# First attention layer of a four-layer kernel: queries, keys and values in one product, a ring of three values, the norm chain two steps into a group

## The reference

```python
qkv = (xin @ Wqkv.T + qkv_bias).reshape(Bs, Lx, 3, H, D)     # H = 16 heads of D = 32
...
sm = jnp.exp(jnp.minimum(scale_mul_log, jnp.log(jnp.float32(100.0))))
qn = q / jnp.maximum(jnp.linalg.norm(q, axis=-1, keepdims=True), 1e-12) * sm
kn = k / jnp.maximum(jnp.linalg.norm(k, axis=-1, keepdims=True), 1e-12)
scores = jnp.einsum('bhqd,bhkd->bhqk', qn, kn) + attn_bias
p = jax.nn.softmax(scores, axis=-1)
o = jnp.einsum('bhqk,bhkd->bhqd', p, v)
...
x = x + attn(_ln(x) * (scale1 + 1.0) + shift1) * gamma1
```

## Time and profile before

| | us |
|---|---|
| median of 3 runs | 2710.25 (2709.88 to 2712.95) |
| profiled execution | 2711.11 |
| its span | 2709.3 |
| TensorE busy | 2364.4 (87%) |
| VectorE busy | 1540.6 (57%) |
| ScalarE busy | 1278.9 (47%) |
| GpSimd busy | 923.5 (34%) |

### The profile page before, as it was taken

One profiled execution on the slowest core, in us unless ns is written; L12 is line 12 of the kernel. 1 busy time (PEld: TensorE's weight loads), 2 busy tenths in 40 slices (PEclk: granted clock), 3 DMA queues, 4 the chain that ended last, 5 costly groups with the idle time before them and its releaser, 6 DMA issues. The chain is left out here.

```text
span 2709.3 us, 45585 instructions
## 1 busy us (share of the span) xinstructions
PE 2364.4 (87%) x15672; PEld 1931.5 (71%) x15672; DVE 1540.6 (57%) x4470; ACT 1278.9 (47%) x3188; POOL 923.5 (34%) x988
## 2 busy tenths in 40 slices
PE   7899999987699997788888788898899999996777
PEld 5787787876578885566666566777788888884565
DVE  5877777785634344656557366547543333334766
ACT  4677777776311112577677366656511111112443
POOL 0344443433767665123323023323111112112331
PEclk8799999999899998677877899999999999997998
DMA  6000000001100002000000100000100000001000
GB/s 258 1 2 6 5 5 6 5 10 45 65 16 32 31 0 73 36 32 1 1 1 2 43 1 1 1 1 1 48 24 24 24 24 23 0 0 51 8 24 32
DMA packets 17084, 65.26 MB, mean 24 GB/s; under 512 B 3292, under 2 KB 4060, under 8 KB 12276
## 3 DMA queue, kind: packets, MB, share of 16 engines
q1 hardware_dynamic: 16884, 62.70, 6.4%
HBM read 57.42 MB, written 5.28 MB: 23 GB/s over the span
## 5 line engine op out<-in xcount | busy, mean ns | idle before, releaser
L2004 POOL TENSOR_TENSOR l2m_hidl<-l2m_hid,l2m_hidh 128x512 fp32r<-128x512 f32 x64 | 100.9, 1577 | 445.6 <-DVE l2m_hidh L1974 445.6
L1869 ACT ACTIVATE l2m_gate<-l2m_psG 128x512 f32<-128x512 f32 x64 | 38.3, 598 | 437.0 <-PE l2m_psU L1800 436.2
L1150 ACT ACTIVATE l0a_prob<-l0a_prob,l0a_nmin 128x512 f32<-128x512 f32 x256 | 184.9, 722 | 58.7 <-DVE l0a_nmin L1431 58.3
L1969 DVE TENSOR_TENSOR l2m_hid<-l2m_gate,l2m_psU 128x512 f32<-128x512 f32 x64 | 44.0, 688 | 281.9 <-ACT l2m_gate L1869 281.9
L1626 POOL TENSOR_TENSOR l0a_prob<-l0a_prob,l0a_rinv 128x512 f32<-128x512 f32 x64 | 67.0, 1047 | 401.9 <-DVE l0a_rinv L1438 401.9
L1162 ACT ACTIVATE l0a_PT<-l0a_psT 128x512 f32<-128x512 f32 x256 | 152.8, 598 | 72.3 <-PE l0a_psT L982 61.7
L1431 DVE CUSTOM_DVE_ANT_0 l0a_prob<-l0a_psS,l0a_mask 128x512 f32<-128x512 f32 x256 | 175.2, 688 | 0.6 <-issue 0.6
L2024 POOL TENSOR_TENSOR res_X<-res_X,l0m_share 128x512 f32<-128x512 f32 x128 | 162.1, 1294 | 24.1 <-DVE l0m_share L1958 22.9
L835 PE MATMUL l0a_psA<-res_l0a_wh,res_hTh 128*128 128x128 f32 (+1 forms) x512 | 151.5, 296 | 19.0 <-ACT l0a_qT L1144 6.8
L1873 ACT ACTIVATE l0m_hid<-l0m_psG,l0m_b1c 128x512 f32<-128x512 f32 x64 | 43.9, 690 | 262.7 <-PE l0m_psG L1800 262.7
L982 PE MATMUL l0a_psT<-res_ident,l0a_prob 128*128 128x128 f32 x1024 | 160.5, 280 | 1.2 <-ACT l0a_PT L1162 0.8
(11 more groups left out here) (410 smaller groups left out, 7642.6 us busy)
## 6 DMA issues: line engine op xcount, KB each, us to landing
res_l2m_stage<-in_l2m_w SPq DMA_DIRECT2D x8, 1536.0 KB, 6.3
res_l0m_stage<-in_l0m_w SPq DMA_DIRECT2D x8, 1024.0 KB, 4.9
cond_w<-in_wmod SPq DMA_DIRECT2D x6, 1024.0 KB, 15.8
res_X<-in_x SPq DMA_DIRECT2D x4, 1024.0 KB, 12.0
l1a_wmod<-in_wmod SPq DMA_DIRECT2D x4, 1024.0 KB, 6.1
out<-res_X SPq DMA_DIRECT2D x16, 256.0 KB, 2.0
l_stage<-in_l_w SPq DMA_DIRECT2D x3, 1024.0 KB, 7.2
cond_stage<-in_l0a_w SPq DMA_DIRECT2D x3, 768.0 KB, 13.8
```

What stands on the lines that cost most here:

```text
L1150: act.activation(prob[:, n % NP, 0:w], src[:, 0:w], ACT.Exp, bias=nmin[:, n % NP:n % NP + 1], scale=-1.0, accum_out=ssum[:, n % NP:n % NP ...
L1969: v.tensor_tensor(hid[:, m, :], gate[:, m, :], psU[m][:], ALU.mult).then_inc(hid_done, 1)
L2004: pool.tensor_tensor(hidl[:, s % 2, m, :], hid[:, m, :], f32(hidh[:, s % 2, m, :]), ALU.subtract).then_inc(hl_done, 1)
```

## The change

Queries, keys and values of a tile become one product of 384 columns. It is cut into two jobs, the first two blocks of channels and the last two, so `proj` has eight halves a group, and both halves use one bank. ScalarE copies 256 columns to `raw` and 128 to `V`, tile by tile. `V` gets three slots, and a copy to a slot waits until the group that used it has been weighed. The tables are new: the halves stand at 7, 7, 8, 8, 11, 11, 16, 16 (group 2), 23, 24, 25, 25, 26, 27, 32, 32 (group 3), 39, 39, 40, 41, 42, 43, 48, 48 (next group 0) and 55, 55, 56, 57, 57, 58, 58, 59 (next group 1). `START` now makes all of groups 0 and 1. The norm chain's bias, squares and sums stand at steps 2, 3 and 4 of every group. The squares go to a tensor of their own place, which lies over `stack`, and wait for the transposes of keys that read it. `xn` holds one tile of rows, and the layer norm's tiles stand at 33, 36, 39 and 42. VectorE drains before each residual.

```diff
-    NORM0 = 7 if L is L0 else LAG + 1
-    NORM_T = (0, 1, 2, 3) if L is L1 else (0, 1, 3, 4)
+    NORM0 = 1 if L is L0 else LAG + 1
+    NORM_T = (0, 3, 6, 9) if L is L0 else (0, 1, 2, 3) if L is L1 else (0, 1, 3, 4)
...
-    VS = 2
+    VS = 3 if L is L0 else 2
...
-        XS = NT if is1 else 2
+        XS = 1 if is0 else NT if is1 else 2
...
+            sq = S.at("sq", [P, NT, QKW], F32, nc.sbuf_base - 4 * NT * SL * NSH * SW)[:]
...
-            sq = xn[:].rearrange("p r c -> p (r c)").rearrange("p (t w) -> p t w", w=QKW)
...
+        PROJ_AT = {2: (7, 7, 8, 8, 11, 11, 16, 16), 3: (23, 24, 25, 25, 26, 27, 32, 32),
...
+        def v_slot(b, hg):
+            return (b * NG + hg) % VS if is0 else hg % VS
...
+        def halved(job):
+            return job[0] == "out" or is0 and job[0] == "proj"
...
-                            sp.wait_ge(v_mm, 2 * NG * B)
...
-                def project(b, hg, t, ps):
-
+                def project(b, hg, x, ps):
+
+                    t, half = divmod(x, 2) if is0 else (x, 1)
...
-                        mm = product(ps, 0, 256, t, lambda w, k: w3(w, hg % NG * GW, 384, k)[:, 0:256])
+                        mm = product(ps, 0, 384, t, lambda w, k: w3(w, hg % NG * GW, 384, k),
+                                     range(2 * half, 2 * half + 2))
...
-                    mm.then_inc(proj_done, 1)
+                    if half:
+                        mm.then_inc(proj_done, 1)
...
-                        freed[i] = [(raw_done, NRAW * (g if is0 else bn) + (x + 1))]
-                    elif kind == "v":
-                        project_v(hg, x, psA[i])
-                        freed[i] = [(v_done, 2 * g + (x // 2 + 1))]
+                        freed[i] = [(v_done, NT * g + (x // 2 + 1)) if is0 else (raw_done, NRAW * bn + (x + 1))]
...
                         act.activation(raw[:, t, hg % 2, :], ps[:, 0:QKW], ACT.Copy).then_inc(raw_done, 1)
+                        if t == 0 and g >= VS:
+                            act.wait_ge(pv_done, U // NG * (g - VS + 1))
+                        act.activation(V[:, v_slot(b, hg), t, :], ps[:, QKW:QKV], ACT.Copy).then_inc(v_done, 1)
...
-                        v.wait_ge(v_mm, 2 * NG * b)
+                        v.wait_ge(proj_done, NT * NG * b)
...
+                    if not start:
+                        v.wait_ge(kT_mm, 4 * (b * NG + hg))
...
+                        v.drain()
                         v.tensor_tensor(xn[:, t % XS, :], ps[:], G[:], ALU.mult)
...
-                        p = s - (2 if hg == NG else 0)
-                        if p == 1:
+                        if s == 2:
                             qk_bias(b, hg)
-                        if p == 2:
-                            qk_squares(hg)
-                        if p == 3:
+                        if s == 3:
+                            qk_squares(b, hg)
+                        if s == 4:
                             qk_norms()
```

More of the change, by code:

```diff
@@ L597, in attention @@
         out_mm, out_done, g_in, xg_done = (S.sem(n) for n in ("out_mm", "out_done", "g_in", "xg_done"))
[L598 to L599 removed]
+        ck_mm, ckh_done, ckl_done, v_done = (S.sem(n) for n in ("ck_mm", "ckh_done", "ckl_done", "v_done"))
         chunks = split_chunks(WCOLS)
@@ L679, in jobs @@
             if hg < NG:
-                if is0 and n in PROJ_AT and (more or PROJ_AT[n][0] < NG):
-                    todo.append(("proj", *PROJ_AT[n]))
-                if is0 and n in V_AT and (more or V_AT[n][0] < NG):
-                    todo.append(("v", *V_AT[n]))
+                if is0:
+                    todo += [("proj", g, x) for g in PROJ_AT if more or g < NG
+                             for x, at in enumerate(PROJ_AT[g]) if at == n]
                 if not is0 and more and hg == NG - 1:
@@ L712, in jobs @@
             return todo
-        START = (([] if PRE else [("norm", 0, t) for t in range(NT)]) + [("proj", 0, t) for t in range(NT)]
+        START = (([] if PRE else [("norm", 0, t) for t in range(NT)])
+                 + [("proj", 0, x) for x in range(2 * NT if is0 else NT)]
                  + ([("ck", 0, 0)] if is1 else [])
-                 + ([("v", 0, t) for t in range(NT)] + [("proj", 1, t) for t in range(NT)] if is0 else
+                 + ([("proj", 1, x) for x in range(2 * NT)] if is0 else
                     [("kv", 0, 0), ("kv", 0, 1)] + ([("far", 0, 0)] if is1 else []))
@@ L720, in attention @@
             START += [("q", 0, j), ("k", 0, j)] if is0 else [("q", 0, j)]
+        def halved(job):
+            return job[0] == "out" or is0 and job[0] == "proj"
         def second(job):
-            return job[0] in ("v", "out") and job[2] % 2 == 1
+            return halved(job) and job[2] % 2 == 1
         def with_banks(todo, last=1, held=None):
@@ L735, in with_banks @@
                     last = 1 - (last if held is None else held)
-                    held = last if job[0] in ("v", "out") else held
+                    held = last if halved(job) else held
                 out.append((job, last))
@@ L829, in latent, with product @@
                     mm.then_inc(ck_mm, 1)
-                def product(ps, c0, n, t, cols):
-                    for k in range(NK):
+                def product(ps, c0, n, t, cols, ks=range(NK)):
+                    for k in ks:
                         for i, (l, r) in enumerate(passes(hTh, hTl, wh, wl)):
@@ L1001, in weigh @@
                             else:
-                                v, rows = V[:, hg % VS, qt if is1 else c, v0:v0 + HD], P
+                                v, rows = V[:, v_slot(b, u // NT), qt if is1 else c, v0:v0 + HD], P
                             mm = pe.matmul(psO[o][row:row + HD, qt * P:(qt + 1) * P],
@@ L1046, in norm_evacuate, with raw_copy @@
                     op.then_inc(hf_done, 1)
-                def raw_copy(b, hg, t, ps, start):
-                    g = b * NG + hg
+                def raw_copy(b, hg, x, ps, start):
+                    g, t = b * NG + hg, x // 2 if is0 else x
                     act.wait_ge(proj_done, (NT * g if is0 else NRAW * (b + (1 if hg == NG else 0))) + (t + 1))
@@ L1121, in run @@
                         act.activation(ckh[:], psA[i][:], ACT.Copy).then_inc(ckh_done, 1)
-                    elif kind == "proj":
+                    elif kind == "proj" and (second(job) or not is0):
                         raw_copy(b, hg, x, psA[i], start)
-                    elif kind == "v" and second(job):
-                        act.wait_ge(v_mm, 2 * g + (x // 2 + 1))
-                        act.activation(V[:, hg % VS, x - 1:x + 1, :],
-                                       psA[i][:, 0:2 * P].rearrange("p (t c) -> p t c", t=2),
-                                       ACT.Copy).then_inc(v_done, 1)
                     elif kind == "kv":
@@ L1291, in qk_bias, with qk_squares @@
                                     qb[:, None, w_hg * P:(w_hg + 1) * P].to_broadcast([P, NT, P]), ALU.add)
-                def qk_squares(hg):
+                def qk_squares(b, hg, start=False):
+                    if not start:
+                        v.wait_ge(kT_mm, 4 * (b * NG + hg))
                     v.drain()
```

16 lines of the change are left out of this document (4 added, 12 removed).

## The result

Measured: 2720.17 us (median of 5 runs, 2718.84 to 2722.35) against 2709.88 for the kernel before (5 runs). The ratio is 1.0041, with a 95% interval of 1.0028 to 1.0054: slower by 10 us, where 20 us less were forecast. The profiled execution took 2721.5 us, its span 2719.7, mean clock 0.913 (before 0.921). The attention layer runs from 42.0 to 683.2 us, 12 us more than before; the later layers gave about 2 back, which is within what repeated runs differ by: from the last score product of this attention to the end the profiles of this case took 2059.5 to 2068.3 us, with the same instructions.

The account below looks back on a forecast made before the run. TensorE was taken to bound the kernel, some 25 us a batch ahead of the next engine. 2 x -7.1 - 4.6 - 6.5 + 1 + 4 = -20.3 us, from 2711.1 to 2690.8; own range 2680 to 2702, range given 2673 to 2707.

Parts of the forecast that it names:

- TensorE's saving: Joined products: 384-column matmuls 0.174 us apart, a tile 2.09 us instead of 2.76, 43 us less over 64 tiles.
- rival C: Matmul spacing goes by columns, so the wide one costs what two narrow did, 0.230; products only change places: 2711; chance 0.03.
- Where the removed work lay: Groups of a middle batch: product time -4.7, +2.7, -5.2, -3.4 counted as -3.5, +2, -3.6, -2, together -7.1 us.
- the three signs of being wrong: Spacing 0.2 or more; batches 1 and 2 over 145 us; half clock in more than one stretch of a batch.
- Before the first batch: Start: wide matmuls on the slow clock delay VectorE's bias 2 us, partly offset by less TensorE work before transposes: +1 us.
- The small edits: Bias place, narrow value copies, bank, drains, value slot and weight transfer: together +4 us.
- the bias wait: VectorE at step 2 of a group waits for ScalarE's copy, 11 times: bounds 0 and 11 us, 1 us extra counted.
- the drain's 0.1 each: VectorE's drain ahead of each of the 16 residuals costs 0.1 us, 1.5 us in all.
- the bank's 0.5 a batch: Bank freed one copy later; jobs at steps 40, 42, 44 take the bank just filled: 0.5 us a batch, 1.5 in all.
- B: VectorE takes it all: bias waits add 11 us, group 2 stays at 42 us; together 22, so 2712; chance 0.12.
- A: TensorE stays the bound throughout and all 43 us come: about 2668; chance 0.08.
- D: Granted clock falls in eleven product-free heads of groups 0, 2 and 3, 3 us each, 33 in all: 2724; chance 0.07.

Follow-up runs that it names:

- the second run of the second set against the first: Kernel before with 384-column products at the old query and key places, later values unused: 2715.63 us; the same with spread norm and residual drains: 2716.07 us.
- the run with 2 of 12 matmuls: Changed kernel, each joined tile after those ahead of the first batch issuing only 2 of its 12 matmuls (results wrong, copies and waits kept): 2692.88 us.
- the fill: Changed kernel with each first-layer score product issued three times in steps without a job, to keep TensorE's clock up: 2716.24 us.
- the four-slot version: Changed kernel with four value slots, half products spread over more steps and the kernel before's narrow start, nothing left out: 2701.62 us.
- the run without the chain: Changed kernel without VectorE's squares, sums, roots and scaling of queries and keys after the first group, TensorE's instructions untouched: 2668.97 us.

## Why the prediction was wrong

**TensorE's saving: right.** Spacing 0.174, a tile 2.09. Columns alone (rival C) would have made the join worth nothing; it is worth 23.7 us in place. The group sums of product time (-4.7, +2.7, -5.2, -3.4) were right as well.

**Where the removed work lay: the step that failed.** It turned the work of a whole group of 16 steps into time with a discount: -3.5, +2, -3.6, -2 and so -7.1 a middle batch, and it had no term for the clock. Measured in batch 1: -1.0, +2.2, -2.2, +0.5 (-0.5); batch 2 came out at +2.9. The kernel couples its engines over a few steps, not 16: score n waits for the minimum n-3, the minimum n for the transposes n-8, which TensorE issues at step n-2. So the balance has to hold within three or four steps. I saw that steps 0 to 6 would become VectorE's and counted 3.5 of 4.7 us as gain (with 10.4 us of VectorE's work, where the earlier trace rows has it busy for 12.5). The gain came (4.6 us in 0-5). What I missed is what the bare steps do to the steps behind them: the tiles stood in steps 7 and 8 behind a VectorE peak instead of beside it, and partly at the half clock: +3.0 in 5-9. The same in 36-42 (+7.1; the spread norm lies there too) and in 53-60 (+6.1 for 1.6 of work). About half of the 16.1 us in these three stretches went when the clock was held up (50.4 to 42.6), so the clock was a term of first size, and not one to put at nothing. Between them 42-48 gave 6.5 back; the half clock of the earlier trace rows stood there before (0.83 in 308.26 to 328.85) and does not after (1.00). Batch 0, forecast at -4.6, came out at +4.4: group 1 alone went from 31.8 to 36.0 us where I had +1. Batch 3, forecast at -6.5, came out at about +2. Two of the three signs of being wrong that I had named came: batches 1 and 2 stayed over 145 us, and the half clock came in three stretches of batch 1.

**Before the first batch:** +1 forecast, +3.5 in the profile (first score 3.1 later, bias at 53.5 against 49.6). The half clock lasted 5.5 us, shown here in a window of the kernel after, in place of the 3.3 of the earlier trace rows:

```profile
42.00:47.50 5.50, 5.48 (x18) 5.50 (x19) 0.00 (x0) 0.55 (x2) 0.00 (x0) 0.53 0.79 235
```

And it was wrong that the eight wide tiles take less of TensorE than the twelve narrow jobs: 96 x 0.174 and 48 x (0.118 + 0.112 + 0.118) are both 16.7.

**The small edits:** the bias wait was bounded at 1.00 a time and is 2.54, three times a batch. Taking it away gave nothing, but that run made the squares dearer at the same time, so what the wait costs stays open. Drains and spread norm cost nothing that shows (the second run of the second set against the first: 0.4 us). For the drain's 0.1 each and the bank's 0.5 a batch the prediction had no row, and no run takes the bank or the narrow copies by itself.

**The rivals.** B named part of the mechanism, that VectorE takes it all, with 22 us given back; in fact over 30 were. A is refuted by the result, and by the run with 2 of 12 matmuls. D, at 0.07, named the other part, and its falls came: the mean clock of the layer went from 0.95 to 0.91, some 25 us of lost full-speed work. TensorE was busy through most of it (in steps 39 to 42 of batch 1 for 8.47 of 8.47 us, at a clock of 0.79). That the fill got back 4 us at most (in the four-slot version nothing) bounds the gain from filling, not the price of the falls. D's 2724 lies near the 2720 measured, but by eleven falls of 3 us each, 33 us, where the lost work of the layer grew by 25; with B's share in it that nearness is in part luck.

**What stays open:** how the loss divides between the fallen clock and the ring of buffers cannot be read off, since the fill that holds the clock up costs work of its own, and the run without the chain raised the clock too. That the spread norm was free was shown beside the old places only; in the changed kernel it lies in the stretch that grew most.
